# Low halves of q and k by TensorE and ScalarE, six of 16 score tiles to ScalarE, four of them halved by an adding transfer

## What is computed

```python
def one_query(qs):                                  # q, k: [b, tok, head, 64]
    return -jnp.sum(jnp.abs(qs[:, None, :, :] - k), axis=-1) * scale
...
v = (x @ wqv_w.T + wqv_b).reshape(b, t, 3 * h, d)
q, vf, vb = (v[:, :, :h], v[:, :, h:2 * h], v[:, :, 2 * h:])
k = x[:, :, None, :] * wk[None, None]
a = _l1_scores(q, k)                                # then a row of zeros is appended
a = jax.nn.softmax(a, axis=1)[:, :t]
bf = jnp.einsum('bsdh,bshw->bdhw', a, vf)
bb = jnp.einsum('bdsh,bshw->bdhw', a, vb)
```

## Time and profile before

| | |
|---|---|
| time, median of 3 runs (lowest, highest) | 2817.27 us (2817.07, 2817.75) |
| the profiled execution | 2817.37 us |
| its span, first to last instruction | 2815.6 us |
| VectorE busy | 2322.0 us (82%) |
| TensorE busy | 2145.3 us (76%) |
| GpSimd busy | 1750.9 us (62%) |
| ScalarE busy | 1380.3 us (49%) |
| VectorE, reductions of D tiles (line 1337) | 1644.1 us, 1408 of 1217 ns |
| stage of the L1 attention | 713 to 2658 us of the span |

### The profile page before, as it was taken

How to read it: one execution, slowest core, us unless ns; L and a number is a source line. 1 busy time by engine, 2 the same in 40 slices (tenths; PEclk the granted TensorE clock), 3 DMA queues, 4 the chain that set the end, 5 groups by cost and what they waited for, 6 DMA issues and landing times.

```text
span 2815.6 us, 43219 instructions
## 1 busy us (share of the span) xinstructions
PE 2145.3 (76%) x11861; PEld 898.4 (32%) x11861; DVE 2322.0 (82%) x2847; ACT 1380.3 (49%) x2997; POOL 1750.9 (62%) x1015
## 2 busy tenths in 40 slices
PE   4649999994777777777777777777777777777466
PEld 3533333331223223223223323223222232232245
DVE  3877778788889889889899899899899899898542
ACT  0325555552455555555555555555555555555234
POOL 0103333232588888887887887887887887887411
PEclk8879999997899999999999999999999999999768
DMA  5100000000111111111111111111111111111000
GB/s 136 44 1 1 1 0 0 0 0 2 49 44 47 46 41 46 47 42 45 47 43 43 47 45 43 47 46 43 45 47 43 44 47 44 43 47 46 16 11 19
DMA packets 163208, 101.96 MB, mean 36 GB/s; under 512 B 55773, under 2 KB 161182, under 8 KB 163039
## 3 DMA queue, kind: packets, MB, share of 16 engines
q1 hardware_dynamic: 162858, 101.41, 14.6%
q10 hardware_dynamic: 316, 0.12, 0.0%
HBM read 10.63 MB, written 4.19 MB: 5 GB/s over the span
## 4 chain that ended last, share of the span: by engine, by line
PE 47%; DVE 29%; issue 16%; ACT 3%; DVEq 2%; DMA 1%; SPq 1%; POOL 1%; ACTq 0%; POOLq 0%
DVE score L1337 21%; PE pp L744 14%; PE pp L593 5%; DVE qk L1316 3%; PE pp L715 3%; PE pp L686 2%; PE pp L614 2%; PE pp L672 2%; PE pp L618 2%; PE pp L615 2%; PE pp L619 2%; PE pp L679 2%; PE pp L585 1%; PE pp L710 1%; ACT vb L966 1%
## 5 line engine op out<-in xcount | busy, mean ns | idle before, releaser
L1337 DVE TENSOR_REDUCE score<-pp 128x16 f32<-128x1024 f32 x1408 | 1644.1, 1217 | 192.5 <-PE pp L744 189.4
L1452 POOL TENSOR_TENSOR absd<-absd 128x2560 f32<-128x2560 f32 (+4 forms) x640 | 1450.1, 2266 | 368.0 <-ACT absd L977 327.9
L744 PE MATMUL pp<-blocks,pick 128*128 128x512 f16 x4096 | 1111.6, 382 | 199.5 <-DVE score L1337 161.8
L977 ACT ACTIVATE absd<-pp 128x1024 f32<-128x1024 f32 x640 | 655.0, 1023 | 712.7 <-PE pp L744 712.7
L744 PEld LDWEIGHTS pp<-blocks,pick 128*128 128x128 f16 x4096 | 316.2, 98 | 852.3 <-DVE score L1337 464.1
L1428 POOL TENSOR_TENSOR absd<-absd,yw 128x512 f32<-128x512 f32 x112 | 142.3, 1270 | 318.9 <-DVE yw L1255 318.9
L916 ACT ACTIVATE absd<-pp 128x512 f32<-128x512 f32 x256 | 150.8, 596 | 148.2 <-PE pp L615 145.7
L1271 DVE SCALAR_TENSOR_TENSOR absd<-pp,absd 128x512 f32<-128x512 f32 x256 | 172.4, 687 | 53.2 <-ACT absd L916 38.6
L989 ACT ACTIVATE expd<-attn 128x65 f32<-128x65 f32 x512 | 155.6, 315 | 0.0
L593 PE MATMUL pp<-absd 128*64 128x512 f32 x512 | 138.1, 618 | 0.0
L672 PE MATMUL pp<-wk_diag,xT 96*128 96x512 f32 x130 | 74.1, 652 | 73.0 <-DVE qk L1316 73.0
(11 more groups left out here) (200 smaller groups left out, 2201.8 us busy)
## 6 DMA issues: line engine op xcount, KB each, us to landing
blocks<-qk SPq DMA_DIRECT2D x1032, 64.0 KB, 2.0
attn<-score SPq DMA_DIRECT2D x1024, 16.0 KB, 1.8
xs<-xn SPq DMA_DIRECT2D x66, 32.0 KB, 1.8
big<-in_wrb_t SPq DMA_DIRECT2D x1, 2064.0 KB
big<-in_x_rows SPq DMA_DIRECT2D x4, 512.0 KB, 6.2
token_rows<-big SPq DMA_DIRECT2D x8, 256.0 KB, 2.0
big<-in_L_ffn_w SPq DMA_DIRECT2D x4, 512.0 KB, 10.0
out<-big SPq DMA_DIRECT2D x16, 128.0 KB, 2.0
```

The lines of the kernel that those rows point to most:

```text
L744: mm = pe.matmul(ps[bank + n], pick[:, unit % 8 + n, :], blocks[:, b, unit // 16, unit // 8 % 2, :], start=True, stop=True)
L977: nc.scalar.activation(absd[odd][:, 16 * u:16 * u + 16, :], pp[:, 4:6, :].rearrange("p n (h w) -> p (n h) w", w=D), ACT.Abs).then_inc(X["a ...
L1337: dve.tensor_reduce(score[:, odd, b, 16 * d:16 * d + 16], pp[:, bank:bank + 2, :].rearrange("p n (h w) -> p (n h) w", w=D), AX.X, ALU.add, ...
L1452: nc.gpsimd.tensor_tensor(x[:, :, 0:w], x[:, :, 0:w], x[:, :, w:2 * w], ALU.add).then_inc(X["tree"], 1)
```

## The change

Six things change, all in the L1 attention but for one buffer.

1. `ORDER` gets a sixth A: 10 D tiles and 6 A tiles for each image. The A tiles stand at 1, 4, 7, 10, 12 and 14.
2. The low halves leave VectorE. TensorE makes the 32-bit product a second time into `ps[6]` and adds to it the high half times a matrix with -2048 on its diagonal (`neg_eye`); ScalarE copies the sum out as the low half. The q one stands after tile 12 of image 0, the k one after tile 0 of image 1.
3. GpSimd's first level is split. A transfer that adds (1 MB, from GpSimd's queue, `halve`) does it for the first four A tiles, as soon as these are there; GpSimd does it for the other two. `absd` is laid out as two halves for it. The transfer of the next image is issued between levels 2 and 3 of the tree of this one, and there GpSimd waits for the fourth A tile of the next image.
4. SyncE sends the blocks of the next pair's image 0 ahead of the scores of image 1.
5. `turn` and `queries` stand one tile later, and VectorE's `finish` and `gated` one tile earlier.
6. `c_cols` of the first stage lies in `absd0`.

```diff
-ORDER = "DADDADDADDADDADD"
+ORDER = "DADDADDADDADADAD"
+NT = 4
@@ SyncE, pair
                 fill_blocks(q, 1, at == 0)
                 if at >= 1:
                     spread(q - 1, 1 - odd, 0, at == 1)
+                fill_blocks(q + 1, 0, False)
+                if at >= 1:
                     spread(q - 1, 1 - odd, 1, at == 1)
-                fill_blocks(q + 1, 0, False)
                 load_pair(following)
@@ TensorE
+            def low(p, odd, kind):
+                pe.wait_ge(X["half"], 4 * p + 2 * kind + 1)
+                if kind:
+                    pe.matmul(ps[6], xT1[:, odd, :], wk_diag[:].rearrange("p h d -> p (h d)"), start=True, stop=False)
+                else:
+                    pe.matmul(ps[6], xTq[:], wqv[:, 0:QK], start=True, stop=False)
+                pe.matmul(ps[6], neg_eye[:], qk[:, kind, 0, :], start=False, stop=True).then_inc(X["klo_ps" if kind else "qlo_ps"], 1)
...
-                        if k == 7:
+                        if k == 8:
                             turn(q + 1, at)
-                        if k == 9:
+                        if k == 10:
                             queries(q + 1, at)
+                        if k == 12:
+                            low(q + 1, 1 - odd, 0)
                         if k == 14:
                             keys(q + 1, 1 - odd)
                     else:
+                        if k == 0:
+                            low(q + 1, 1 - odd, 1)
@@ ScalarE
+            def low(p, kind):
+                act.wait_ge(X["klo_ps" if kind else "qlo_ps"], p + 1)
+                nc.scalar.copy(qk[:, kind, 1, :], ps[6]).then_inc(X["half"], 1)
...
-                nc.scalar.activation(absd[odd][:, 16 * u:16 * u + 16, :], pp[:, 4:6, :].rearrange("p n (h w) -> p (n h) w", w=D),
-                                     ACT.Abs).then_inc(X["abs"], 1)
+                nc.scalar.activation(absd[odd][:, :, 16 * u:16 * u + 16, :].rearrange("p c n w -> p n c w"),
+                                     pp[:, 4:6, :].rearrange("p n (h c w) -> p (n h) c w", c=2, w=D // 2), ACT.Abs).then_inc(X["abs"], 1)
...
                 high_q(q + 1, False)
+                low(q + 1, 0)
                 absolute(s, 0, 4, first)
+                absolute(s, 0, 5, first)
                 s += 1
                 high_k(q + 1)
+                low(q + 1, 1)
...
                 absolute(s, 1, 4, first)
                 if at >= 1:
                     exponentials(q - 1, 1, at == 1)
+                absolute(s, 1, 5, first)
@@ VectorE
-            def low(p, kind):
-                dve.wait_ge(X["half"], 4 * p + 2 * kind + 1)
-                dve.scalar_tensor_tensor(out=qk[:, kind, 1, :], in0=qk[:, kind, 0, :], scalar=-LO_SCALE, in1=ps[6],
-                                         op0=ALU.mult, op1=ALU.add).then_inc(X["half"], 1)
...
-                        if b == 0 and d == 4 and at >= 3:
+                        if b == 0 and d == 3 and at >= 3:
                             finish(q - 3, slot)
-                        if b == 0 and d == 8:
-                            low(q + 1, 0)
-                        if b == 1 and d == 1:
-                            low(q + 1, 1)
-                        if b == 1 and d == 8 and at >= 2:
+                        if b == 1 and d == 7 and at >= 2:
                             gated(q - 2)
@@ GpSimd
-                x = absd[b]
-                pool.wait_ge(X["abs"], NA * (s + 1))
-                for m, w in enumerate((32, 16, 8, 4, 2)):
...
+            def halve(s, p, b):
+                pool.wait_ge(X["abs"], NA * s + NT)
+                pool.sem_inc(X["taken"], 1)
+                pool.dma_start(absd[b][:, 0, 0:16 * NT, :].rearrange("p n w -> p (n w)"),
+                               absd[b][:, 1, 0:16 * NT, :].rearrange("p n w -> p (n w)"),
+                               accum_op=ALU.add).then_inc(X[f"half{b}"], 16)
...
+                x = absd[b][:, 0]
+                rest = slice(16 * NT, 16 * NA)
                 pool.wait_ge(X["abs"], NA * (s + 1))
+                nc.gpsimd.tensor_tensor(x[:, rest, :], x[:, rest, :], absd[b][:, 1, rest, :], ALU.add).then_inc(X["tree"], 1)
+                pool.wait_ge(X[f"half{b}"], 16 * (p + 1))
+                level(s, x, 1, 16)
+                level(s, x, 2, 8)
+                if following:
+                    halve(s + 1, p + b, 1 - b)
+                level(s, x, 3, 4)
+                level(s, x, 4, 2)
```

More of the change, by code:

```diff
@@ L182, in build @@
         pick = sb("pick", [P, 8, P], F16)
+        neg_eye = sb("neg_eye", [P, P], F16)
         xs1 = sb("xs1", [P, 2 * D])
@@ L243, in build @@
         tok_rows = big[:].rearrange("p (u n) -> p u n", u=8)
-        absd = [t[:].rearrange("p (n w) -> p n w", w=D) for t in (absd0, absd1)]
+        absd = [t[:].rearrange("p (c n w) -> p c n w", c=2, w=D // 2) for t in (absd0, absd1)]
         wk_b = big[0:D, 0:QK].rearrange("p (h d) -> p h d", d=D)
@@ L264, in build @@
         X = {n: sem("d_" + n) for n in (
-            "xs", "wk_in", "consts", "xT_ps", "xT_sb", "xTq", "q_ps", "k_ps", "half", "tb0", "tb1",
-            "diffD", "diffA", "red", "abs", "tree", "pooled", "spread0", "spread1", "exp", "zr", "attk", "attq_ps", "attq",
+            "xs", "wk_in", "consts", "xT_ps", "xT_sb", "xTq", "q_ps", "k_ps", "qlo_ps", "klo_ps", "half", "tb0", "tb1",
+            "diffD", "diffA", "red", "abs", "taken", "half0", "half1", "tree", "pooled", "spread0", "spread1", "exp", "zr", "attk", "attq_ps", "attq",
             "o_ps", "tanh", "y", "yT_ps", "yT", "fan_ps", "hx", "sum", "vb_ps", "vb", "vf_ps", "vf")}
@@ L735, in image @@
                             pe.wait_ge(X["red"], ND * s + d - 1)
-                        unit, bank, done = 2 * d, 2 * ((b + d) % 2), "diffD"
+                        unit, bank, done = 2 * d, 2 * (d % 2), "diffD"
                         d += 1
@@ L777, in _ @@
             queries(0, 0)
+            low(0, 0, 0)
             keys(0, 0)
+            low(0, 0, 1)
             for q in range(4):
@@ L1040, in _ @@
             high_q(0, True)
+            low(0, 0)
             high_k(0)
+            low(0, 1)
             for q in range(4):
@@ L1443, in _, with level, batch @@
             nc.gpsimd.tensor_tensor(h[:], h[:], xn[:, 0:PAIRS, :], ALU.add).then_inc(X["hx"], 1)
-            def batch(s, p, odd, b, at):
-                x = absd[b]
-                pool.wait_ge(X["abs"], NA * (s + 1))
-                for m, w in enumerate((32, 16, 8, 4, 2)):
-                    if m:
-                        pool.wait_ge(X["tree"], 5 * s + m)
-                    nc.gpsimd.tensor_tensor(x[:, :, 0:w], x[:, :, 0:w], x[:, :, w:2 * w], ALU.add).then_inc(X["tree"], 1)
+            def halve(s, p, b):
[4 more added lines that the diff above has]
+                               accum_op=ALU.add).then_inc(X[f"half{b}"], 16)
+            def level(s, x, m, w):
+                pool.wait_ge(X["tree"], 5 * s + m)
+                nc.gpsimd.tensor_tensor(x[:, :, 0:w], x[:, :, 0:w], x[:, :, w:2 * w], ALU.add).then_inc(X["tree"], 1)
+            def batch(s, p, odd, b, at, following):
+                x = absd[b][:, 0]
+                rest = slice(16 * NT, 16 * NA)
+                pool.wait_ge(X["abs"], NA * (s + 1))
+                nc.gpsimd.tensor_tensor(x[:, rest, :], x[:, rest, :], absd[b][:, 1, rest, :], ALU.add).then_inc(X["tree"], 1)
[6 more added lines that the diff above has]
+                level(s, x, 4, 2)
                 pool.wait_ge(X["tree"], 5 * s + 5)
@@ L1478, in _ @@
             last = PAIRS - 1
-            batch(2 * last + 1, last, 1, 1, 4)
+            batch(2 * last + 1, last, 1, 1, 4, False)
             normalise(last - 1, False)
```

16 lines of the change are left out of this document (8 added, 8 removed).

## The result

| | before | with the change |
|---|---|---|
| median of 4 runs (lowest, highest) | 2817.17 us (2816.85, 2817.75) | 2958.43 us (2955.06, 2959.11) |
| the profiled execution, its span | 2817.37 us, 2815.6 us | 2958.07 us, 2956.2 us |

The change makes the kernel slower by a factor of 1.0499 (95% interval 1.0481 to 1.0517), by 141 us. The forecast was 2868 us, +51, in a range up to 2912: the sign is right, the size is not.

A forecast was written before the change was run, and what follows sets the result against it. VectorE, 27 us of 29.8 a pair, was the bound; with the change 14.33 + 16.06 = 30.39, with 0.22 30.61 us a pair, 0.80 more, times 64 = +51: 2868 us. Range 2824 to 2910 (0.60); 2776 to 2912 about 0.8.

The forecast's parts named there:

- the late scores: Image 1's scores, queued behind the next blocks, land at 11.4 us; ScalarE, ready at 10.05, idles before its exponentials.
- The step on which the sign hangs: SyncE's new order: scores sent behind the blocks land late, so ScalarE stands idle 1.35 us before the exponentials.
- The step that failed: TensorE's work from tile 14 of image 1 on: 17 tiles at 0.43 us each, 7.31 us.
- The 0.16 that it gives to times above 2910 us: Rival: the adding transfer bounds the pair if its issue-to-landing time passes 9.9 us; 3010 us at 11; chance 0.16.
- The mis-sized term: TensorE's second product and 16-bit matmul for each low half: 1.08 us each, between 0.9 and 1.3.
- scores in time: Rival: no 1.35 us stall before the exponentials; 29.24 us a pair, 2781 us in all; chance 0.18.
- The base: Time of a pair in the kernel before: 29.81 us, from 369 reductions in 500 us, 22 to a pair.
- The layout of the old order: Check of the costing on the kernel before: 29.59 us a pair, with the missing 0.22 carried along.
- What left VectorE: Two reductions of 1.17 us and two low halves of 0.68 leave VectorE: 3.5 us of a pair.
- The adding transfer: GpSimd's new transfer lands 7.2 us after its issue, and is hidden up to 9.9.

The follow-up runs named there:

- e1: The changed kernel with SyncE's old queue order (scores of image 1 ahead of the next blocks): 2804.83 us, 0.9954 of the kernel before.
- e3: The changed kernel with 20 unused turns of the identity on TensorE ahead of the late tile 14 of image 1: 2892.25 us, 1.0276.
- e6: The changed kernel with 10 unused turns of the identity on TensorE ahead of tile 14 of image 1: 2894.17 us, 1.028 (three executions).
- e9: The changed kernel with the old queue order and the old 11 D and 5 A tiles, low halves moved and adding transfer kept: 2735.3 us, 0.9723.

## Why the prediction was right in its sign and wrong in its size

The 141 us come apart like this, each part by the runs and as it was forecast:

| part | runs | measured | forecast |
|---|---|---|---|
| everything but the late scores and the clock | e1 less before | -12 us | -36 us |
| the late scores | e3 less e1 | +87 us | +88 us (1.37 x 64) |
| TensorE's clock | the change less e3 | +66 us | 0 |
| together | | +141 us | +51 us |

**The step on which the sign hangs** held. The forecast has the scores landed 11.4 us after the last D tile's reduction, ScalarE ready at 10.05, a stall of 1.35; measured are 1.20 in the pair shown, and 1.23 on average (18.4 us in 15 pairs). The waits of TensorE at tile 14 were to be about 1.2 to 1.4 in image 0 and over 2 us in image 1, and are 1.17 and 2.49. Counted from the same point, the scores landed after 11.8 us and ScalarE was ready after 10.6: both came later than laid out, and the difference stayed, which is some luck: it is the difference of two sums that were each off by 0.4 to 0.6. Without the stall, in e1, the wait at tile 14 of image 1 is 1.19.

**The step that failed** is one that has no line in the sum: it takes every TensorE step behind the wait from rows at full clock. All its rows were, because no gap in the loop of the kernel before comes near 2.5 us; the longest between 800 and 2500 us is the 1.54 of the earlier trace rows. The sum itself put a gap of over 2 us into each pair and then went on with 0.43 us a tile. Measured, the three tiles behind it take 2.74 us instead of 1.46, and `values_f` lasts 830 ns a matmul instead of 592: 1.16 us a pair (32.13 less 30.97), 66 of the 90 us by which the forecast is off. A row for it stood among those shown: in the earlier trace rows sixteen matmuls behind 4.64 us of idleness take 6.23 us, 0.78 a tile where the loop has 0.43. The forecast read that row for SyncE's landing time and not for its duration; the window 713 to 718 us of the kernel before has a clock of 0.50. That row does not tell whether 2.5 us are enough (35.1 us of idleness, up to 701.92, stand a little ahead of its 4.64), but it was a rival with a place and a price, and the forecast has none for it. The 0.16 that it gives to times above 2910 us are for the adding transfer, which the runs clear, so they don't stand for this. The Trainium skill, "TensorE: Matmul & The Clock Gate" (Part 1), says that the half clock is TensorE's default and that its recent activity releases the full one. The trace agrees: 0.50 behind the 2.49 us, 1.00 with turns in their place.

**The mis-sized term** is the second product, "0.86 and half a tile 0.22, so 1.08 us each". It measures 0.97 and 0.22 (1504.10 to 1505.07 to 1505.29, and again 1509.26 to 1510.22), 1.19 each. Each second product waits for ScalarE's copy of the high half (done at 1504.05 and 1509.20). The nearer row was `keys`, which also starts behind a wait, at 0.97, and not the 0.86 of `values_f`, which follows a tile. Twice 0.11 is 0.22 us a pair, 14 us of the 24 by which e1 missed the forecast of "scores in time". The steady pairs hold no more than that: e1's is 0.33 shorter than the one before, where 0.57 was forecast, 0.24 in 64 pairs. Where the other 10 lie no run shows.

**The base** was 0.2 too low. 369 reductions in 500 us are 22 a pair only if none is missing from the records; by GpSimd's landmark a pair takes 30.01 us, not 29.81. The layout of the old order then missed 0.42 and not 0.22. Since the same is missing on both sides, it cancels in the difference.

**What left VectorE** went as costed: 20 reductions a pair of 1.22 us, no low halves. Its idle time is 8.1 us a pair (126 in 15.6 pairs), against 7 forecast; with full clock, in e1, it is 5.9. **The adding transfer** was put at 7.2 us from its issue on GpSimd, hidden up to 9.9. It lands after 7.0 by the page, and in e1 the level behind it starts 7.4 after the issue (1517.11 to 1524.54).
**What it didn't ask.** It priced the sixth tile as a reduction taken off VectorE and an absolute value added to ScalarE. The runs show its cost in TensorE's queue, where A tiles two apart share one pair of banks: 70 us, 54 of them by place alone. The low halves, which the forecast sees as one of several gains, are the only part of the change tried here that gains, 92 us; VectorE's `finish` and `gated` one tile earlier were not tried alone.

## What to carry to other kernels

When a change makes one long wait for TensorE, price what stands behind the wait at the half clock too, and compare the new gap with the longest that the trace already has: here 1.2 to 1.5 us were nearly always free and 2.5 cost another 1.2 us each pair. Cheap unused matmuls in such a gap test this in one run. An engine that is late costs nothing until someone needs its next result: with the next A tile four tiles off 1.2 us of lateness were free, and with it two tiles off they cost 87 us, and the clock 66 more.

## What the runs showed of the hardware that was not expected

- TensorE's granted clock fell from 2.4 to 1.2 GHz within an idle stretch of 2.49 us, before its end, though the 16 us ahead of it were 86% busy (13.71 of 16.00), and was back at full some 3 us after work resumed. It fell in 40 of 53 pairs with such a gap, and in e6 at gaps of 2.05 and 2.54 us, but not at its two of 1.79 and 1.80. The usual gaps of e1 (1.19) and e6 (1.42) left it at full but for 4 of some 57 in e1. So the length of the gap alone did not decide.
- Ten unused 32-bit turns of 128 x 128, 1.25 us, in that gap held the full clock as well as twenty, but for the two places where more than 2 us of the gap were left.
- A transfer that adds 1 MB from on-chip memory to on-chip memory lands 7.0 us after its issue, beside 64 KB and 16 KB copies that still land after 2.0 and 1.8, as before (medians; in e9 the adding transfer's is 7.4).
- A 32-bit product of 512 columns took a step of 0.96 to 0.97 us where it started behind a wait (1502.93 before, 1504.10 and 1509.26 with the change), and 0.86 to 0.87 where it followed other work (1518.88 before, 1502.25 and 1507.49 with the change). That the wait is the reason is not shown.
